# Reordering an attention kernel's streams, with direct modulation products for three heads

## What is computed

```python
mod = (_silu(L0_c) @ L0_wmod).reshape(L0_c.shape[0], 6, 1, -1)
sa, ca, ga, sb, cb, gb = (mod[:, 0], mod[:, 1], ...)
ga = (2 * (ga >= 0) - 1) * jnp.maximum(jnp.abs(ga), 0.25)
h = _layernorm(x, axis=-1) * (1 + ca) + sa
x = x + ga * _L0_attn_ref(h, ...)
h = _layernorm(x, axis=-1) * (1 + cb) + sb
x = x + gb * _L0_ffn_ref(h, ...)
```

```python
q = q * cos + _rotate_half(q) * sin
k = k * cos + _rotate_half(k) * sin
scores = jnp.einsum('bhgtd,bhkd->bhgtk', qg, k) / math.sqrt(DH)
scores = jnp.where(causal, scores, jnp.finfo(jnp.float32).min)
ctx = jnp.einsum('bhgtk,bhkd->bhgtd', softmax(scores), v)
```

## Time and profile before

| | us |
|---|---|
| median of three executions | 783.2 |
| lowest, highest | 782.6, 783.42 |
| the profiled execution: time | 784.32 |
| the profiled execution: span | 782.4 |
| mean granted TensorE clock in it | 0.985 |
| busy: PE, DVE, POOL, ACT | 718.6, 476.8, 337.9, 319.6 |

### The profile page before, as it was taken

One profiled execution on the slowest core, in us unless ns is written; L12 is line 12 of the kernel. 1 busy time (PEld: TensorE's weight loads), 2 busy tenths in 40 slices (PEclk: granted clock), 3 DMA queues, 4 the chain that ended last, 5 costly groups with the idle time before them and its releaser, 6 DMA issues.

```text
span 782.4 us, 10145 instructions
## 1 busy us (share of the span) xinstructions
PE 718.6 (92%) x3646; PEld 429.1 (55%) x3646; DVE 476.8 (61%) x716; ACT 319.6 (41%) x536; POOL 337.9 (43%) x275
## 2 busy tenths in 40 slices
PE   4897898879999999888999999999869999999998
PEld 2343433223333433217778888744437788887886
DVE  3858777657777877505876547686985433337311
ACT  4311266556666666772134511264424233233100
POOL 0327993785654755282436622312732221224400
PEclk9998899989999999999999999999999999999999
DMA  9452524250505410302013210024020111111111
GB/s 318 157 120 73 118 109 62 101 117 4 118 20 101 85 37 1 98 28 96 14 26 90 72 41 0 1 101 85 0 68 1 54 33 48 54 54 54 41 68 40
DMA packets 24111, 52.99 MB, mean 68 GB/s; under 512 B 4253, under 2 KB 8101, under 8 KB 23045
## 3 DMA queue, kind: packets, MB, share of 16 engines
q1 hardware_dynamic: 24068, 52.44, 24.6%
HBM read 45.63 MB, written 6.60 MB: 67 GB/s over the span
## 4 chain that ended last, share of the span: by engine, by line
PE 67%; DVE 11%; issue 8%; POOL 8%; DMA 3%; ACT 2%; SPq 1%; ACTq 0%; DVEq 0%; POOLq 0%
PE ps L863 65%; DVE mxp L1786 3%; POOL x L2322 1%; ACT pr L1432 1%; DVE st L1628 1%; DMA rq<-in_mask 1%; POOL wsum L2207 1%; PE ps L880 1%; POOL pr L2223 1%; POOL arena L2327 1%; DMA wmr<-in_wmr 1%; DVE xnb L1652 1%; DVE x L1866 1%; POOL wmr L2205 1%; PE ps L1029 1%
## 5 line engine op out<-in xcount | busy, mean ns | idle before, releaser
L863 PE MATMUL ps<-arena 128*128 128x512 f32 (+1 forms) x1404 | 326.4, 392 | 3.7 <-POOL arena L2146 1.9
L863 PEld LDWEIGHTS ps<-arena 128*128 128x128 f32 (+1 forms) x1404 | 259.6, 186 | 62.2 <-POOL arena L2146 2.3
L1786 DVE TENSOR_REDUCE mxp<-ps 128x2 f32<-128x1024 f32 (+3 forms) x160 | 172.8, 1115 | 57.2 <-PE ps L863 55.6
L1432 ACT ACTIVATE pr<-ps 128x512 f32<-128x512 f32 x288 | 162.3, 596 | 89.2 <-PE ps L863 86.9
L863 PE MATMUL ps<-Qst,Kst 99*128 99x512 bf16 x288 | 102.8, 387 | 9.6 <-ACT pr L1432 7.4
L863 PE MATMUL ps<-Kst,Qst 96*128 96x512 bf16 (+3 forms) x384 | 102.0, 337 | 8.2 <-DVE mxp L1786 4.9
L2223 POOL TENSOR_TENSOR pr<-pr,cap 128x512 int32<-128x512 int32 x56 | 70.8, 1279 | 34.9 <-ACT pr L1432 34.6
L863 PE MATMUL ps<-pr,vr 128*32 128x512 f32 x576 | 77.4, 610 | 6.2 <-POOL pr L2223 5.5
L863 PEld LDWEIGHTS ps<-Kst,Qst 96*128 96x128 bf16 x384 | 36.1, 99 | 66.8 <-DVE mxp L1786 27.1
L863 PEld LDWEIGHTS ps<-Qst,Kst 99*128 99x128 bf16 x288 | 26.6, 97 | 83.0 <-ACT pr L1432 60.9
L2327 POOL TENSOR_TENSOR arena<-raw,arena 128x1024 fp32r<-128x1024 f32 x11 | 26.7, 2430 | 88.5 <-ACT arena L1506 83.8
(11 more groups left out here) (201 smaller groups left out, 814.3 us busy)
## 6 DMA issues: line engine op xcount, KB each, us to landing
wmr<-in_wmr SPq DMA_DIRECT2D x8, 1280.0 KB, 11.6
raw<-in_w SPq DMA_DIRECT2D x16, 512.0 KB, 3.2
Qst<-q_parts SPq DMA_DIRECT2D x42, 128.0 KB
q_parts<-qparts SPq DMA_DIRECT2D x3, 768.0 KB, 3.5
x<-in_x SPq DMA_DIRECT2D x8, 256.0 KB, 6.4
wm<-in_wm SPq DMA_DIRECT2D x4, 512.0 KB, 6.5
raw<-in_up SPq DMA_DIRECT2D x8, 256.0 KB, 2.6
raw<-in_down SPq DMA_DIRECT2D x8, 256.0 KB, 2.7
```

The source lines that it names most:

```text
L863: return nc.tensor.matmul(outp, lhs, rhs, start=start, stop=stop, skip_group_check=True)
L1432: A(pr[:, k % PRING, :], ps[:, 4 + k % 2, :], ACT.Exp, scale=float(DH) ** -0.5).then_inc(exp_done, 1)
L1786: V.tensor_reduce(mxp[:, kh, g0:g0 + heads, i].rearrange("p (b e) -> p b e", e=per), units, AXX, ALU.max)\
```

## The change

1. For heads 0, 1 and 2 (MOD_BY_PE = 3) the modulation row comes straight from the weights: 4 chunks x 4 column groups of products against silu(c), without POOL. wmr has two buffers; the first two loads are issued behind the lora matrix's load, the next behind the store of a head's row (heads 0 to 2) or behind its weighing. The lora parts on POOL move behind the work of head 6.
2. Preamble: the identity is loaded ahead of wm0; the first norm's turns stand around the last chunk of mod0; POOL's second sine product comes ahead of key_lo; values(0) comes ahead of the second turn and queries(1, 0) ahead of the scores. POOL's rotation of query chunks 2 and 3 waits for the maxima of head 0, and later for its own buffer; DVE's shuffles for it (`swap_queries`) move.
3. Head 0: the halves of projections stand after units 0, 1, 3, 5, 7, 9, 11, 14, 17 and 19; the two halves of queries(3, 1) ahead of head 1's units 0 and 1.
4. Score units in the bodies are placed by a table of numbers instead of by the costs: 0, 1, 4, 5, 6, 9, 10, 13, 13, 15, 17, 18, 20, 22, maxima at 25, units ahead at 26, 29, 29, 31, 33, 34.
5. modT: DVE's copy stands ahead of the split of the first half and gives the bank free; ACT waits for modc_ready.
6. Mixer: DVE's fd(1,0) is split around scale(0,1); POOL's out(1,1) stands ahead of w13(1,1).
7. Last norm: the products of h1 and h3 with the high part stand ahead of those of both with the low part.

```diff
-             ("centred", 0, 1), ("dg", 0, 1), ("fd", 1, 0), ("scale", 0, 1), ("rest", 0, 0), ("merge", 0, 0),
+             ("centred", 0, 1), ("dg", 0, 1), ("fd_first", 1, 0), ("scale", 0, 1), ("fd_second", 1, 0), ("rest", 0, 0), ("merge", 0, 0),
...
-              ("w13", 1, 1), ("out", 1, 1)]
+              ("out", 1, 1), ("w13", 1, 1)]
...
-FILL = (("v", 1), ("q", 1, 0), ("q", 1, 1), ("q", 2, 0), ("q", 2, 1))
-VT_AT = 11
+FILL = (("q", 1, 1), ("v", 1), ("q", 2, 0), ("q", 2, 1), ("q", 3, 0))
+FILL_AT = (0, 1, 3, 5, 7, 9, 11, 14, 17, 19)
+VT_AT = 8
+MOD_BY_PE = 3
+SCORES_AT = (0, 1, 4, 5, 6, 9, 10, 13, 13, 15, 17, 18, 20, 22)
+CONTEXT_AT = 3
+MAXIMA_AT = 25
+AHEAD_AT = (26, 29, 29, 31, 33, 34)
...
             def mod_step(h):
                 pe.wait_ge(s_read, slots_before(h, NS + 1) - 1)
-                pe.wait_ge(wsum_ready, h + 1)
                 w = MODW // 4
+                if h < MOD_BY_PE:
+                    pe.wait_ge(wmr_in[h % 2], 16 * (h // 2) + 16)
+                    for kc in range(KC):
+                        for q in range(4):
+                            last = mm(ps[32 * q:32 * q + 32, 2, 0:w], sc32[:, kc, :, :].rearrange("p l m -> p (l m)"),
+                                      wmr[h % 2][:, kc, w * q:w * q + w], kc == 0, kc == KC - 1)
+                    last.then_inc(s_full, 1)
+                    return
+                pe.wait_ge(wsum_ready, h - MOD_BY_PE + 1)
...
             def head_dmas(h):
-                if h < NKV - 1:
-                    sp.wait_ge(wsum_ready, h + 1)
-                    sp.dma_start(wmr[:, :, :].rearrange("p c n -> p (c n)"), a["wmr"][h + 1]).then_inc(wmr_in, 16)
+                if MOD_BY_PE <= h < NKV - 2:
+                    sp.wait_ge(wsum_ready, h - MOD_BY_PE + 1)
+                    load_mod(h + 2)
...
+                if h < MOD_BY_PE:
+                    load_mod(h + 2)
...
             for hf in range(2):
                 pool.wait_ge(trig_in[hf], 32)
                 sines(2 * hf)
+                sines(2 * hf + 1)
                 key_lo(hf)
-                sines(2 * hf + 1)
...
             head_v(0)
-            weigh(0)
+            pool.wait_ge(mt_parts, 1)
             rope_queries(2)
-            weigh(1)
             rope_queries(3)
...
             max_turn(0)
-            queries(3, 0)
             mod_step(0)
             pe.wait_ge(st_in[1], 144)
             for s in range(AHEAD):
+                if s < 2:
+                    queries(3, 1, range(2 * s, 2 * s + 2))
                 s_unit(1, s)
-                if s in (1, 3):
-                    queries(3, 1, range(s - 1, s + 1))
...
             ctx_norm(NKV - 1)
+            b = filled(dve, "modT")
+            V.tensor_copy(modc[:, :], ps[:, b, 0:40]).then_inc(read_b[b], 1)
             for c in range(KC):
                 split_lo(c, ("aT", 0, c), aTr[0][:, c, tok[0]], aTr[1][:, c, tok[0]])
-            b = filled(dve, "modT")
-            link(V.tensor_copy(modc[:, :], ps[:, b, 0:40]))
...
+            def gated_fresh(name, piece, slot, hf):
+                weights(pe, piece)
+                bs = [bank_of(pe, (kind, *name, hf)) for kind in ("h1", "h3")]
+                last = first_after_ln(3, hf, [(ps[:, b, :], [w[:, which, :, :] for w in W13[slot]])
+                                              for which, b in enumerate(bs)])
...
             ln_turn(3, 0)
-            gated(("F", 0), ("w13", 0), 0, (0,), fresh=True, whiches=(0,))
+            gated_fresh(("F", 0), ("w13", 0), 0, 0)
             ln_turn(3, 1)
-            gated(("F", 0), ("w13", 0), 0, (0,), whiches=(1,))
```

More of the change, by code:

```diff
@@ L872, in hilo, with ln_turn @@
                 return f(pair[0]), f(pair[1])
-            def ln_turn(L, hf):
+            def ln_turn(L, hf, chunks=range(KC)):
                 pe.wait_ge(ln_xn, 8 * L + 4 * hf + 4)
-                for c in range(KC):
+                for c in chunks:
                     b = bank_of(pe, ("ln", L, hf, c))
@@ L954, in _ @@
             queries(0, 1)
-            values(0)
+            queries(1, 0)
             def s_unit(h, s):
@@ L1063, in _ @@
                 s_unit(0, s)
-                if s < 2 * len(FILL):
-                    job, half = FILL[s // 2], range(2 * (s % 2), 2 * (s % 2) + 2)
-                    if job[0] == "v":
-                        values(job[1], half)
-                    else:
-                        queries(*job[1:], half)
+                for at, (job, half) in zip(FILL_AT, FILL_HALVES):
+                    if at == s:
+                        if job[0] == "v":
+                            values(job[1], half)
+                        else:
+                            queries(*job[1:], half)
                 if s == VT_AT:
@@ L1821, in head_body @@
             def head_body(n, nxt, nxt2, ctx):
-                for _, what, d, s in body_steps(nxt, nxt2, ctx):
+                for k, (_, what, d, s) in enumerate(body_steps(nxt, nxt2, ctx)):
+                    if n == 0 and k == 2:
+                        swap_queries(3)
                     if what == "s":
```

151 lines of the change are left out of this document (75 added, 76 removed).

## The result

The changed kernel takes 758.19 us (four executions, 757.68 to 758.74) against 783.31: a ratio of 0.9678, 95% interval 0.9661 to 0.9696, or 25.1 us less. The forecast was 755 in a range of 749 to 765, and 29.0 us less. The profiled execution took 758.74, with a span of 756.9; the spans differ by 25.5. One execution in this study, of the kernel with the lora parts back, took 1801 us and is left out of its median.

The account below looks back on a forecast made before the run. TensorE, busy 92% of the span, was taken as the bound, with gains where it idles or is slowed, first in attention. Terms 6.2 + 4.5 + 2.3 + 7.2 + 3.9 + 0.4 + 1.3 + 0 + 3.2 = 29.0 gave 755 us, range 749 to 765.

Parts of the forecast that it names:

- Body 2 (7.2): Head body 2: with two weight buffers and lora parts later, the weights and mask stalls go; 37.6 to 30.4 us.
- bodies 3 to 5 (3.9): Even head bodies: units issued where PE waited for ScalarE; 1.3 us gained in each.
- Rival B: Even bodies: the unit table brings nothing, PE's waits only change place; 1.3 x 4 lost, 760.5 us; chance 0.14.
- Body 1 (2.3): Head body 1: weighing no longer stands between POOL's masks; 34.4 to 32.1 us, with 0.8 charged for meeting maxima.
- body 6 (0.4): Head body 6: 30.4 us would become 29.3 + 0.2, less 0.5 charged for POOL's lora parts meeting its maxima.
- Body 0 (4.5): Head body 0: lower clock at 94.9 to 98.3 us goes, maxima collisions shrink, new unit table; 37.1 to 32.6 us.
- Rival A: Start stretch: 72 to 82 us stays at half clock, PE still waiting for DVE's maxima; 760.5 us; chance 0.15.
- Start stretch (6.2): Start to first transposed unit: preamble 2.5, head 0 2.7, maxima and units ahead 1.0; 90.6 to 84.4 us.
- rival E: Head 2's or 3's weights arrive late and POOL or PE waits, 5 to 7 us kept; 761 us; chance 0.05.
- Mixer (0, range -0.3 to +1.95): Mixer's dg: root ahead of w13 splits frees PE's 1.90 us wait unless dg collides with POOL; fd split 0.
- Last norm (3.2): Last norm: twelve h3 matmuls (2.64 us) fill PE's waits for low parts, 0.5 from fuller clock; lower bound 1.8.
- Rival D: Bodies: bunched score units make PE wait for DVE's score slots, 6.4 us a body; slower, 810 us; chance 0.03.

Follow-up runs that it names:

- the earlier shuffle: Changed kernel with DVE's shuffle of query chunk 2 right behind head 0's maxima instead of between head 1's units 2 and 3: 753.33 us.
- both tables: Changed kernel with the mixer orders of DVE and POOL (MIXER_DVE and MIXER_POOL) as they were before the change: 756.84 us.
- POOL's table back: Changed kernel with only POOL's mixer order as before, w13(1,1) ahead of out(1,1), DVE's split of fd kept: 757.16 us.
- the new mixer order: Changed kernel with DVE's second rest moved from ahead of dg(1,0) to ahead of dg(1,1), and POOL's w13(1,1) waiting until dg(1,1) is made: 754.22 us.

## Why the prediction was right, and where it was not

**What bounds.** Right: the gains lie in the attention block, 23.8 of 25.5 us by the traces, where the prediction had 24.5 of 29.0. On medians the whole is 25.1. Head 0's new placing, the early loads and modT were not taken back in a run of their own; their shares are read from their stretches.

**Body 2 (7.2) and bodies 3 to 5 (3.9).** Right in mechanism and size: 7.35 and 4.23. The placing of units with row durations gave 30.2 for an even body; it is 30.26 or 30.27 in every kernel of the study with the new table, and 31.67 with the old one, where it gave 31.5. Rival B argued from PE's 91.9 busy of 95.0 us, and fell: of the 4.23 us only 1.8 were idle time in the view (3.16 to 1.38), the rest stood in matmuls counted as busy. A busy share close to full is no bound for what an order can give.

**Body 1 (2.3) and body 6 (0.4).** 3.3 and 1.4. The mis-sized terms are the charges of 0.8 ("weighing for head 3 may meet the maxima") and 0.5 ("the lora parts on POOL can meet its maxima"). Both came and cost next to nothing. Weighing stood beside the maxima of head 2, which took 2.4 us instead of 2.1. The lora parts met those of head 7, where one step took 1.54 us instead of 0.28; yet body 6 takes 29.05 with them there and 29.06 without, in the kernel that has them back at head 2. So the 1.3 us that this step of the maxima lost reached nothing.

**Body 0 (4.5).** 2.5. The step that failed is "the lower clock goes". It went at 94.9 to 98.3 and came at 84.1 to 94.4, and costs 2.3 (34.55 against 32.2). Without it the body would have been 0.4 shorter than forecast. The charge for a collision (the sum has 0.65 of it, 5.4 - 0.65 - 0.2, half of 1.3 and not of the 2.6 named above it) was too high: here POOL's rotation ended at 109.3, 0.4 us ahead of the maxima, and in the kernel with the lora parts back, at the upper clock, they met (3.6 us instead of 2.1) in a body of 32.2, where the kernel with the earlier shuffle, without a collision, has 32.0. Rival A had a half clock behind the maxima of head 0, with the place too early; that PE's waiting brings it about, as it says, isn't shown. The prediction's own sign of being wrong, half clock in the start stretch, did turn up, for its last 1.5 us.

**Start stretch (6.2).** 5.0. PE's first score came at 42.85, not at 41.8; in the 12 kernels of this study that start alike on PE it lies between 41.6 and 42.9. Their first product with weights starts at 8.3 to 10.0 us, which may be a part of that; the two don't go together in every trace. From the first score to head 0's last reduction it took 29.4 us where it had been 34.4, 5.0 less; the two terms together had said 4.7 for that (5.2 less the 0.5 of the earlier score). The preamble's term (2.5) was mis-sized: the first reduction came 1.2 earlier, since three DVE instructions beside POOL's moved work took 0.8 us longer each, and of these 1.2 only 0.6 was kept to the end of head 0. The third term (1.0, 12.7 us to 11.7 from head 0's last reduction to the first transposed unit) gave 0.6: it took 12.1, and 11.6 in the kernels whose clock was not at half there. "PE keeps its full clock" is what failed in it.

**Direct products (0.9 each).** 0.83, taken from body 1 with and without one. Head 2's and 3's weights were there in time; rival E fell.

**modT (1.3).** 1.5.

**Mixer (0, range -0.3 to +1.95).** Wrong: -2.8, of which 2.4 come back with both tables. The step on dg(1,1) held in its mechanism: the root came free, and then 2.1 us of collision with the first split of w13; PE's second dg came 0.8 later behind the first than before, where -0.3 was the bound, with half clock on the products between the two. The step that failed is "the split of fd on DVE lies in a stretch without DVE idle time: 0". It gave PE 1.09 us (hof is there earlier), but DVE waited 0.5 for PE inside the new order, and its next steps on x ran beside POOL's for 6.79 instead of 5.95 us; since DVE is full there, all of this, 1.3 us, arrives at dg(1,0), where PE, being early, now stood 2.54. The kernel with POOL's table back has the same 6.79 and loses just these 1.3. The other 1.5 came with POOL's order, on which half clock also lay. An edit in a stretch where an engine is full is not free; it is charged in full at the next hand-over.

**The price of a collision.** dg took 2.82 us beside a POOL split of 2.34 and 0.69 without, and hof 2.92 against 0.75 when the split was moved onto it. The Trainium skill ("SBUF — State Buffer", the two separate sides) has a DVE instruction with two SBUF inputs and a GpSimd instruction that reads SBUF exclude each other for a whole instruction; both rows agree. By the full price in the maxima the prediction would have been 757. But of the maxima only those of head 7 paid much in the changed kernel, off the path, and the mixer, for which I had it too cheap, did.

**Last norm (3.2).** 3.4, with the two terms mis-sized against each other: the order gave 1.75, not 2.64, since the products with the high part that now stand ahead make the front 1.0 longer; the clock gave 1.65, not 0.5. The order's part is at the lower bound that was named (1.8).

**Rival D** fell: PE waited 4.2 us for DVE ahead of score units in the whole kernel, all of it in the start stretch, and nothing in bodies 0 to 6 with the pairs in one step.

## What to carry to other kernels

Place a hand-written order step by step with the durations of its own trace, with each reader's queue and buffer, before trying it: that gave the length of an even body within 0.1 us under the new table and within 0.2 under the old, where the busy shares suggested that little was left. Price a move on an engine that is full by where its next hand-over stands, and ask of every moved instruction on GpSimd what VectorE does at that time. And measure an edit by its own stretch in the trace, beside the total: stretches of half clock of 3 to 10 us move between executions and edits and are as large as the effects.

## What the runs showed of the hardware that was not expected

The granted clock fell to half at places that differ between kernels with the same code up to there: in body 0 for 10.3, 3.4, 6.9 or 0 us. In the profiled executions there was a stretch of half clock in or behind the mixer in every kernel; the four with the new mixer order had one, and the others one to three. In the seven kernels where PE stood 2.5 us for the first of the last two dg, a half clock began 0.2 to 1.8 us behind that wait; in the seven without the wait none began within 4 us of it. But a wait doesn't always bring it: a wait of 1.94 us for hof stands in the kernel before and in that with both tables back, and the clock fell behind it in the second alone. Which waits bring it about is open: it would need the same kernel's traces many times over.
